# The last result rows of an attention + mixture-of-experts layer: weighed on ScalarE and summed on GpSimd instead of multiplied by diagonal tiles on TensorE

## The reference, cut to what matters

```python
x = _layernorm(x + attention(x))                       # x1 below
probs = jax.nn.softmax(x @ w_gate, axis=-1)
topk_w, topk_ids = jax.lax.top_k(probs, 2)
topk_w = topk_w / jnp.sum(topk_w, axis=-1, keepdims=True)
gu = jnp.einsum('th,ehf->etf', x, w_gate_up)
eo = jnp.einsum('eti,eih->eth', _silu_and_mul(gu), w_down)
routed = jnp.einsum('te,eth->th', combine, eo)         # combine: the two weights of each token
shared = _silu_and_mul(x @ w_sh_gate_up) @ w_sh_down
out = _layernorm(x + routed + shared)
```

## Time and profile before

| what | us |
|---|---|
| median of three runs (lowest, highest) | 235.03 (232.92, 236.46) |
| the execution that was profiled | 232.75 |
| its span, first to last instruction | 230.9 |
| TensorE busy | 218.6 |
| VectorE busy | 151.6 |
| GpSimd busy | 133.6 |
| ScalarE busy | 116.6 |

### The profile page before, as it was taken

One profiled execution on the slowest core, in us unless ns is written; L12 is line 12 of the kernel. 1 busy time (PEld: TensorE's weight loads), 2 busy tenths in 40 slices (PEclk: granted clock), 3 DMA queues, 4 the chain that ended last, 5 costly groups with the idle time before them and its releaser, 6 DMA issues.

```text
span 230.9 us, 4976 instructions
## 1 busy us (share of the span) xinstructions
PE 218.6 (95%) x1428; PEld 191.0 (83%) x1428; DVE 151.6 (66%) x530; ACT 116.6 (50%) x300; POOL 133.6 (58%) x152
## 2 busy tenths in 40 slices
PE   7899999999999999999999989999999999999781
PEld 2468888879888978978799879999999988888681
DVE  2771553525975593865998886666666742689975
ACT  2273441591266083257307177777777763312393
POOL 0047697899877978477678006666666774003300
PEclk9999999999999999999999999999999999999999
DMA  5973484333131122022255246666666520973036
GB/s 154 375 236 88 109 303 125 94 92 91 44 95 47 49 92 93 0 93 93 92 183 185 58 107 173 186 165 178 178 178 180 147 95 4 374 232 123 0 134 232
DMA packets 21404, 31.59 MB, mean 137 GB/s; under 512 B 3200, under 2 KB 14081, under 8 KB 21380
## 3 DMA queue, kind: packets, MB, share of 16 engines
q1 hardware_dynamic: 17424, 22.33, 32.6%
q0 software_dynamic: 3408, 8.43, 10.4%
q10 hardware_dynamic: 548, 0.53, 0.8%
HBM read 19.56 MB, written 12.62 MB: 139 GB/s over the span
## 4 chain that ended last, share of the span: by engine, by line
PE 79%; DVE 11%; ACT 4%; DMA 3%; issue 2%; SPq 0%; DVEq 0%; ACTq 0%
PE bank L339 18%; PE bank L341 17%; PE bank L340 16%; PE bank L639 4%; PE bank L381 3%; PE bank L540 3%; DMA xt_raw<-in_xT 3%; PE bank L666 2%; PE bank L459 2%; PE bank L669 2%; PE bank L667 2%; PE bank L395 2%; DVE x L1281 2%; PE bank L657 2%; PE bank L448 2%
## 5 line engine op out<-in xcount | busy, mean ns | idle before, releaser
L1441 POOL DMA_INDIRECT y_pairs<-x_t,dst x39 | 38.0, 973 | 28.0 <-DVE dst L1174 24.1
L1404 POOL DMA_INDIRECT x_slots<-x,slot x32 | 32.3, 1010 | 10.2 <-issue 9.0
L339 PE MATMUL bank<-x1t_hi,wf_hi 128*128 128x512 f32 x64 | 26.2, 410 | 0.7 <-DVE xt_raw L1091 0.5
L339 PE MATMUL bank<-wf_hi,ot_hi 128*128 x78 | 25.3, 324 | 0.4 <-DVE ot_lo L1176 0.4
L341 PE MATMUL bank<-x1t_hi,wf_lo 128*128 128x512 f32 x64 | 25.3, 395 | 0.0
L340 PE MATMUL bank<-x1t_lo,wf_hi 128*128 128x512 f32 x64 | 25.2, 394 | 0.0
L1385 POOL TENSOR_TENSOR wf_lo<-stage,wf_hi 128x512 fp32r<-128x512 f32 x18 | 23.2, 1289 | 1.4
L756 ACT ACTIVATE k_sb<-bank,cst 128x256 f32<-128x256 f32 x16 | 7.7, 481 | 29.6 <-PE bank L356 27.1
L341 PE MATMUL bank<-wf_hi,ot_lo 128*128 x78 | 22.0, 282 | 0.0
L340 PE MATMUL bank<-wf_lo,ot_hi 128*128 x78 | 21.9, 280 | 0.0
L1174 DVE SCALAR_TENSOR_TENSOR dst<-o_sb,te_f 128x1 f32 (+1 forms) x39 | 8.5, 219 | 16.0 <-ACT ot_hi L870 15.9
(11 more groups left out here) (185 smaller groups left out, 685.0 us busy)
## 6 DMA issues: line engine op xcount, KB each, us to landing
o_sb<-x_slots SPq DMA_DIRECT2D x39, 129.0 KB
stage<-in_wffn SPq DMA_DIRECT2D x18, 256.0 KB, 2.7
x<-in_x SPq DMA_DIRECT2D x4, 512.0 KB, 6.8
out<-x SPq DMA_DIRECT2D x7, 256.0 KB, 2.5
xt_raw<-in_xT SPq DMA_DIRECT2D x3, 512.0 KB, 6.7
x_slots<-fill SPq DMA_DIRECT2D x9, 129.0 KB, 2.9
x<-in_watt SPq DMA_DIRECT2D x4, 256.0 KB, 6.0
k_sb<-y_pairs SPq DMA_DIRECT2D x2, 512.0 KB, 3.9
```

What stands on the lines that cost most here:

```text
L339: mm(o, w_hi, m_hi, start=start, stop=False, **more)
L1404: pool.indirect_dma_start(out=x_scat, out_offset=bass.IndirectOffsetOnAxis(ap=slot[:, j, t:t + 1], axis=0), in_=x1[:, t, :], in_offset=Non ...
L1441: pool.indirect_dma_start(out=y_scat, out_offset=bass.IndirectOffsetOnAxis(ap=dst[:, j:j + 1], axis=0), in_=ey[:, u, :], in_offset=None, b ...
```

## The change

ScalarE multiplies the result rows of three pairs by their weights, in place (`weigh`, four instructions of 128x256 a pair), and GpSimd adds them to x1 (`sum_rows`, two instructions of 128x2x256 a pair, one for each expert). The pairs are 6 and 7 (batch 3) and 5 (the last pair of batch 2). So VectorE has no `combine(5)` any more, `last_rows` is one identity product a tile, and the diagonal tiles are gone. The pairs are loaded in the order 6, 7, 5, 0, 1, 2, 3, 4; the loads of 2, 3 and 4 wait for the sums of 6, 7 and 5. `shared_dn(3,0)` takes its two tiles quarter by quarter, and waits for each quarter by itself. VectorE's end is put in another order.

```diff
+        first_pairs = (6, 7, 5)
+        pair_order = first_pairs + (0, 1, 2, 3, 4)
+        pair = [free[pair_order.index(n) % n_pair][:, 0] for n in range(T // UNIT)]
...
-            for n in range(T // UNIT):
-                if n >= n_pair:
-                    sp.wait_ge(S["acc_out"], UNIT * (n - n_pair + 1))
+            for at, n in enumerate(pair_order):
+                if at >= n_pair:
+                    sp.wait_ge(S["sum_out"], at - n_pair + 1)
...
             def last_rows(t):
-                pe.wait_ge(pair_in[i // UNIT], 16)
-                for j in range(TOPK):
-                    mm(o, diag[:, t, j, :], pair[i // UNIT][:, i % UNIT, j, :], start=(j == 0), stop=False)
-                mm(o, ident, x1[:, i, 0:D], start=False, stop=False)
+                pe.wait_ge(S["sum_out"], t // UNIT + 1)
+                mm(o, ident, x1[:, i, 0:D], start=True, stop=False)
...
+                if b == NB - 1 and h == 0:
+                    order = [(t, c) for c in range(CS) for t in both]
+                for t, c in order:
+                    if b == NB - 1 and order[0] == (0, 0) and t == 0:
+                        pe.wait_ge(S["shh_out"], CS * b + c + 1)
+                        pe.wait_ge(S["shl_out"], CS * b + c + 1)
...
+            def weigh(n):
+                act.wait_ge(pair_in[n], 16)
+                for i in range(UNIT):
+                    for j in range(TOPK):
+                        at = n * UNIT + i
+                        y = pair[n][:, i, j, :]
+                        activation(y, y, ACT.Identity, scale=w_top[:, j, at:at + 1]).then_inc(S["wy_out"], 1)
...
+            shared_sg(3, 0)
+            act.wait_ge(S["wtop_out"], 1)
+            weigh(first_pairs[0])
+            shared_hh(3, 0)
+            weigh(first_pairs[1])
+            weigh(first_pairs[2])
+            for c in range(1, CS):
+                shared_sg(3, c)
+                shared_hh(3, c)
...
-            for t in range(TB):
-                for j in range(TOPK):
-                    i = T - TB + t
-                    v.tensor_scalar(diag[:, t, j, :], ident, w_top[:, j, i:i + 1], None, ALU.mult
-                                    ).then_inc(S["diag_out"], 1)
...
-            h_and_lo(3, 0)
+            shared_h(3, 0)
             combine(0)
             shared_out(2, 0)
+            shared_lo(3, 0)
             combine(1)
             shared_out(2, 1)
+            last_moments(0, range(TB))
             combine(2)
             shared_h(3, 1)
-            last_moments(0, range(TB))
+            combine(3)
             shared_lo(3, 1)
-            combine(3)
             shared_h(3, 2)
             last_moments(1, range(TB))
+            shared_h(3, 3)
             shared_lo(3, 2)
+            shared_lo(3, 3)
             combine(4)
-            shared_h(3, 3)
-            combine(5)
-            shared_lo(3, 3)
...
             apply_norm(3, 0)
+            last_moments(3, range(3, 4))
             apply_norm(3, 1)
-            last_moments(3, range(3, 4))
...
+            def sum_rows(at):
+                n = first_pairs[at]
+                pool.wait_ge(S["wy_out"], UNIT * TOPK * (at + 1))
+                if n < (NB - 1) * TB // UNIT:
+                    pool.wait_ge(S["sres_out"], n + 1)
+                else:
+                    pool.wait_ge(S[f"scattered{NB - 1}"], 16 * TOPK * TB)
+                r = x1[:, n * UNIT:(n + 1) * UNIT, 0:D]
+                link(g.tensor_tensor(r, pair[n][:, :, 0, :], r, ALU.add))
+                g.tensor_tensor(r, pair[n][:, :, 1, :], r, ALU.add).then_inc(S["sum_out"], 1)
+
+            for at in range(len(first_pairs)):
+                sum_rows(at)
```

32 lines of the change are left out of this document (16 added, 16 removed).

## The result

| | before | after |
|---|---|---|
| median of three runs, us (lowest, highest) | 235.03 (232.92, 236.46) | 237.56 (235.99, 237.79) |
| the execution that was profiled, us | 232.75 | 237.56 |
| its span, us | 230.9 | 235.8 |
| mean granted clock | 0.998 | 0.976 |

The two profiled executions differ by 4.9 us of span, the medians by 2.5 only; the text comes back to this.

A forecast was written before the change was run, and what follows sets the result against it. The end was bound by VectorE's order up to `shared_h(3,3)`, then ScalarE's tail. `shared_h(3,1)` at 216.2 plus 18.2 plus 0.9 for the clock gave a span of 235.3, hence a 239.4 us median; 8-in-10 range 234.0 to 242.0.

The forecast's parts named there:

- The diagonal tiles count 0: Ahead of the first expert tile: dropping 8 instructions, 1.65 us of VectorE, gains 0, bounds 0 and -0.4.
- The diagonal products count 0: TensorE's `last_rows` at the end: four tiles take 3.4 us less, but this gains 0.
- Pair 0 lands 6.5 us after its load: Loads at the end: pair 0, now fourth, lands at 202.6, so `combine(0)` waits until then instead of beginning at 200.83.
- The sum without exclusion, 0.8 us sooner: End of the kernel: if sums and combines run side by side, `shared_h(3,1)` ends at 211.9 and the span at 230.1.
- They take turns, and it is a whole wait: GpSimd's sums and VectorE's combines ahead of `shared_h(3,1)` exclude each other, adding 4.3 us, bounds 0 and 4.6.
- VectorE's instructions with one input in SBUF, and the statistics, stay free: Beside GpSimd's sums, `shared_out`, `shared_h` and the statistics do not contend for the port and are charged no wait.
- `shared_h(3,1)` ends near 216: VectorE's end: this product ends at 216.2, from 211.9 plus 4.3 us of waiting; before, it ended at 208.5.
- TensorE's stop of 6.4 us costs the clock, 0.9 us: Ahead of `shared_gu(3,3)`: the stop drops TensorE to 1.2 GHz, costing between 0 and 1.7 us, middle 0.9.
- The median is 2.28 above the sum: Last step: the median was put 2.28 us above the profiled execution, taking 237.15 to 239.4 us.
- The rival of VectorE going first: GpSimd gets the port only in gaps between VectorE's two-input instructions; median 236.2 to 236.9 us, chance 0.22.
- No exclusion: Rival: GpSimd's sums run beside VectorE's combines, `combine(0)` begins at 202.6; median 234.2 us, 0.8 faster, chance 0.18.
- The clock staying low through the down products: Rival: TensorE at half rate through `shared_gu(3,3)`, identities and all down products; end 240.6, median 244.7 us, chance 0.06.

The follow-up runs named there:

- e2: Changed kernel with GpSimd's sums replaced by four memsets a pair into an unused tile; 235.21 us in one execution, end 31.34 us after `shared_h(3,0)` starts.
- e3: Changed kernel with twenty idle matmuls ahead of `shared_gu(3,3)` to keep TensorE busy; ratio 1.0098 to the kernel before, median 237.21 us against 234.06.
- e1: Changed kernel with GpSimd's six sums left out, only the semaphore raised; one execution took 235.95 us, beside a median of 234.06 of the kernel before.
- e6: Changed kernel with pair 0 loaded first and 6, 7, 5 behind it; one execution took 263.6 us, beside a median of 261.60 of the kernel before.
- e4: Changed kernel with `shared_h(3,1)` moved ahead of batch 0's statistics and `combine(2)`; ratio 1.0093 to the kernel before.
- e7: Changed kernel again, without an edit, where everything takes about 260 us; median 265.35 us against 261.60 for the kernel before, ratio 1.0174.
- e9: Kernel before again, unedited, as a control where everything takes about 260 us; ratio 0.9863, median 260.12 us against 262.35.
- e10: Changed kernel with pair 0 loaded first and `shared_h(3,1)` ahead of batch 0's statistics and `combine(2)`; ratio 1.0053 to the kernel before.

## Why the prediction came out as it did

From the spans: the forecast had 235.3 for the end, 4.4 us later than before, and it is 235.8, 4.9 later. Those 4.9 us, by the mark of `shared_h(3,0)`:

| part | us | from |
|---|---|---|
| the end starts later | +1.19 | 200.03 − 198.84 |
| new order, pair 0 fourth, no turns, clock at 1.00 | −0.72 | e2: 31.34 − 32.06 |
| VectorE and GpSimd take turns | +2.67 | e3 − e2: 34.01 − 31.34 |
| TensorE at 1.2 GHz through `shared_gu(3,3)` | +1.76 | after − e3: 35.77 − 34.01 |
| together | +4.90 | 235.8 − 230.9 |

Step by step:

- *The diagonal tiles count 0.* Right. The 1.65 us are gone, and no wait of TensorE for them was there to go.
- *The diagonal products count 0, since TensorE doesn't set the end.* Right: with the sums' price and the clock's gone (e2), the end is set by VectorE's order and ScalarE's tail.
- *Pair 0 lands 6.5 us after its load.* Right: its load is issued at 197.39 and takes 6.2 us, and `combine(0)` waits 2.92 us for it.
- *The sum without exclusion, 0.8 us sooner.* Right to 0.1 (e2).
- *They take turns, and it is a whole wait.* The mechanism is right, by e1 and e2 and by the single instructions. The term was mis-sized: 4.3 us predicted, 2.8 measured at the combines (3.84 − 1.79 and 2.52 − 1.78) and 2.7 at the end. Two inputs of it were off. The weighing goes in steps of 0.40 us (four in 1.70), where I had taken 0.50 from the normalizations, and the sums take 1.18 to 1.19 us, where I had 1.28. So pair 6 was nearly summed when pair 0 had landed; I had a whole microsecond of waiting there. And turns are not paid in full: `combine(0)` is 2.05 us longer beside the last 0.49 us of pair 6's sums and the 2.64 us of pair 7's, for which I had charged 1.0 and 2.25.
- *VectorE's instructions with one input in SBUF, and the statistics, stay free.* Right: the statistics take 1.39 with a sum beside them from 211.13, and in e6 `shared_out` takes 0.69 from 230.48 with a sum from 230.91.
- *`shared_h(3,1)` ends near 216.* It ended at 215.76, but by a smaller term and a later start: 15.04 us after `shared_h(3,0)` where the forecast had 16.7.
- *TensorE's stop of 6.4 us costs the clock, 0.9 us.* The fall is right, though the stop was 4.69. The size was half: 1.76, since the lower level lasted through the whole quarter, just over the upper bound (1.7). The second profile had 0.73.
- *12.2 us from the last high part to the end.* 235.8 − (222.69 + 0.62) = 12.5.
- *The median is 2.28 above the sum.* This step failed. The sum was made against the profiled execution of before, 232.75, which lies below all three timed runs; I moved the result up by the same distance. The profiled execution of the changed kernel is its median, 237.56. Without that step the forecast would have been 237.15. Of the 2.28 about 1.0 was itself the scatter of three runs: the 19 beside e1 to e4, which also take about 235 us, have a median of 234.06, 1.3 above that execution. The 2.5 us between the two medians of three is no firmer; e7's median is 3.75 above that of before, so that 237.15 would have come so near is luck too. The distance was a property of one execution, not of the kernel: e9 shows a part of what it can consist of, 1.4 us for the clock at the stop of 2.29 us, which the profiled execution of before did not pay; and the expert tiles scatter by more.

So the forecast was 1.8 us high and the increase in the span 0.5 us low, and the near hit of the end comes in part from errors that cancel: the turns 1.6 us too dear, the clock 0.9 too cheap, and 1.2 us of a later start that the forecast did not have and no experiment explains.

Is that later start chance? For it speak the four equal programs whose first loads lie 4.7 us apart. Against it speaks the table: where all takes 260 us, `shared_h(3,0)` starts at 224.80 to 226.94 in the five profiles of kernels with the work of before, and at 227.58 to 230.66 in the three with the work moved; of the five with it moved that take about 235 us, only e4's (198.22) does not start later than before's 198.84. And TensorE's wait for the tokens' transfers is 0.3 or 0.4 us in all six profiles with the work of before, and 0.6 to 2.1 in all eight with it moved. Some 0.3 us of that costs nothing, since without the diagonal tiles the first expert tile is reached sooner (its wait ends at 135.58 instead of 135.91, though it is 0.66 us long instead of 0.30). So a part of the later start may belong to the change; the cause stays open.

The rival of VectorE going first is out: VectorE's instructions are the ones that grow, GpSimd's 1.19 grows to 1.38 at most in the changed kernel and to 1.53 in e10. No exclusion is out by e1 and e2. The clock staying low through the down products was not seen.

## What to carry to other kernels

Work that is moved to an idle engine is paid for by what it locks: two-input sums on GpSimd beside two-input work on VectorE take VectorE's time, so such work belongs beside instructions that read PSUM or one operand, and here the reordering without the move is the better half of the change. When an end hangs on a wait of TensorE of two microseconds and more, count the clock's fall as a matter of chance and price it from both outcomes. And a sum against one profiled execution forecasts that execution's like; the distance from there to a median should be explained, or left out.
